# Second routed layer's rows and results in one DRAM buffer, sixteen early tiles, twenty stores on GpSimd, three gathers under way

## What is computed

```
raw_gate = softmax(einsum('btd,de->bte', x, gate))
_, topk_idx = top_k(raw_gate, 3)                      # of 16 experts
gate_topk = raw_gate where chosen, normed to sum 1
hidden = relu(einsum('btd,edh->bteh', x, W1) + b1)    # h = 256
expert_out = einsum('bteh,ehd->bted', hidden, W2) + b2
out = einsum('bte,bted->btd', gate_topk, expert_out)
x = x + out
```

## Time and profile before

| | us |
|---|---|
| median of 3 runs | 539.93 (538.46 to 541.28) |
| the profiled execution's own time | 540.01 |
| its span in the trace | 538.3 |
| PE busy | 415.3 (77%) |
| DVE busy | 336.5 (63%) |
| ACT busy | 240.1 (45%) |
| GpSimd (POOL) busy | 221.6 (41%) |

### The profile page before, as it was taken

The page is one execution under the profiler, slowest core; times in us unless marked ns, Lnnn a source line. Parts: engine busy times, 40 slices in busy tenths (PEclk is TensorE's granted clock), DMA queues, the critical chain, the costliest instruction groups (busy, mean ns, idle before and its releaser), DMA issues.

```text
span 538.3 us, 10062 instructions
## 1 busy us (share of the span) xinstructions
PE 415.3 (77%) x2628; PEld 344.9 (64%) x2628; DVE 336.5 (63%) x1143; ACT 240.1 (45%) x635; POOL 221.6 (41%) x276
## 2 busy tenths in 40 slices
PE   5887869999899888667899927763999999963450
PEld 5866758887676787357889915543767857752340
DVE  6656545654777767223444526667747588768887
ACT  1332316555344531444667713542566565742321
POOL 3511760035413777750215567554212254451215
PEclk9697559999798967577999968978999999995555
DMA  7999646892190111242336522110000000000002
GB/s 199 306 406 407 148 142 211 290 318 80 43 378 20 45 40 45 73 129 83 115 108 164 152 57 68 40 34 6 1 2 0 1 2 1 1 1 1 0 1 78
DMA packets 64421, 56.48 MB, mean 105 GB/s; under 512 B 12178, under 2 KB 50542, under 8 KB 64238
## 3 DMA queue, kind: packets, MB, share of 16 engines
q1 hardware_dynamic: 57534, 45.61, 25.9%
q0 software_dynamic: 4288, 8.79, 5.2%
q10 hardware_dynamic: 2544, 1.44, 0.9%
HBM read 24.10 MB, written 31.72 MB: 104 GB/s over the span
## 4 chain that ended last, share of the span: by engine, by line
PE 30%; DMA 18%; DVE 18%; POOL 13%; issue 10%; ACT 5%; DVEq 4%; SPq 1%; POOLq 0%; ACTq 0%
POOL rowbuf L645 8%; DMA vZ<-outbuf,slots 5%; PE bank L2104 4%; DMA rowbuf<-h_sb,slots 4%; PE bank L2250 4%; PE bank L2263 4%; DMA h_sb<-outbuf,slots 3%; PE bank L2120 3%; PE bank L2109 2%; POOL rstd L622 2%; PE bank L1959 2%; DMA wall<-outbuf,slots 2%; ACT xn L1631 2%; DVE stats L825 1%; DVE x L1285 1%
## 5 line engine op out<-in xcount | busy, mean ns | idle before, releaser
L1725 ACT ACTIVATE r<-bank,b 128x128 f32<-128x128 f32 x218 | 66.3, 366 | 36.1 <-PE bank L2250 35.3
L622 POOL TENSOR_TENSOR rstd<-veps,mhalf 128x4 f32<-128x4 f32 x32 | 33.8, 1057 | 110.4 <-DVE veps L830 110.1
L2263 PE MATMUL bank<-wall,r 128*128 x436 | 69.5, 293 | 11.9 <-DVE h_sb L1298 10.9
L645 POOL DMA_INDIRECT rowbuf<-h_sb,slots x64 | 63.0, 985 | 34.0 <-DMA rowbuf<-h_sb,slots 15.5
L2263 PEld LDWEIGHTS bank<-wall,r 128*128 128x128 f32 x436 | 59.1, 202 | 14.6 <-issue 12.8
L672 POOL DMA_INDIRECT vZ<-outbuf,slots x40 | 38.7, 968 | 60.5 <-DMA outbuf<-h_sb 35.8
L2250 PE MATMUL bank<-on,e_sb 128*128 128x128 f32 x348 | 58.4, 300 | 0.0
L2120 PE MATMUL bank<-vB,eT 128*128 128x36 f32 x384 | 50.8, 282 | 0.0
L2120 PEld LDWEIGHTS bank<-vB,eT 128*128 128x128 f32 x384 | 50.8, 206 | 0.0
L2250 PEld LDWEIGHTS bank<-on,e_sb 128*128 128x128 f32 x348 | 49.7, 210 | 0.1
L1298 DVE TENSOR_TENSOR h_sb<-bank,b2all 128x128 f32<-128x128 f32 x86 | 24.8, 290 | 38.0 <-PE bank L2263 36.4
(11 more groups left out here) (304 smaller groups left out, 840.1 us busy)
## 6 DMA issues: line engine op xcount, KB each, us to landing
outbuf<-zero SPq DMA_DIRECT2D x17, 1024.0 KB, 13.3
wall<-in_w SPq DMA_DIRECT2D x4, 2048.0 KB, 12.3
h_sb<-rowbuf SPq DMA_DIRECT2D x86, 64.0 KB, 2.1
outbuf<-h_sb SPq DMA_DIRECT2D x80, 64.0 KB, 2.1
rowbuf<-zero SPq DMA_DIRECT2D x24, 64.0 KB, 1.5
x<-in_x ACTq DMA_DIRECT2D x4, 256.0 KB, 5.6
rowbuf<-h_sb,slots POOLq DMA_INDIRECT x64, 2.2
b2all<-in_L_ffn_b SPq DMA_DIRECT2D x1, 1024.0 KB, 13.8
```

Of the source, the lines that this page charges most:

```text
L622: r = nc.gpsimd.tensor_tensor(rstd[:, at], veps[:, at], mhalf[:, 0:W], ALU.pow)
L645: placed = nc.gpsimd.indirect_dma_start(rowbuf[0:MOE[l][0] * REGION * P], bass.IndirectOffsetOnAxis(slots[:, k * T + t:k * T + t + 1], 0), ...
L1725: i = a.activation(hT[:, u * 512 + c * P:u * 512 + (c + 1) * P], bank[2 + u][:, c * P:(c + 1) * P], ACT.Relu, bias=b1[l][:, bass.ds(e * C ...
L2263: y = mm(bank[6 + s % 2][:, 0:P], hT[:, (s % 2) * 512 + c * P:(s % 2) * 512 + (c + 1) * P], wall[:, bass.ds(e * n + (WHALF + c * P), P)], ...
```

## The change

- In layer 3 the scattered rows go to `outbuf`, too (`rows_of[3]`): a slot's tile is loaded from there and its result is stored back to the same place. The zero tails of layer 3 fall away, since `outbuf` is cleared or holds finished rows of layer 1; before its first scatter of layer 3 GpSimd waits for layer 1's last gathers, the clears and `s_past`.
- `EARLY[3]` goes from 8 to 16, with `FROM[3]`, `LISTED[3]` and `TURNED[3]` later in step, and `PRIOR[3][0]` from 27 to 31.
- GpSimd stores slots 12 to 31 (20 of them) in place of 11, 13, ... 21 (6), and reads their list entries ten at a time.
- Layer 3's gathers wait for the third before them, not the second; scatters wait as before, with semaphores of their own.
- In layer 1, SP waits for the zero tails right after issuing them, ahead of the list read.

```diff
-PRIOR = {1: (11, 15, 19, 23), 3: (27, 39, 51, 63)}
-SHARE = range(11, 23, 2)
-EARLY = {1: 4, 3: 8}
+PRIOR = {1: (11, 15, 19, 23), 3: (31, 39, 51, 63)}
+SHARE = range(12, 32)
+UNDER_WAY = {1: 2, 3: 3}
+EARLY = {1: 4, 3: 16}
...
-FROM = {1: 3, 3: 4}
+FROM = {1: 3, 3: 8}
...
-LISTED = {1: (1, 2), 3: (1, 2)}
-TURNED = {1: 0, 3: 0}
+LISTED = {1: (1, 2), 3: (3, 6)}
+TURNED = {1: 0, 3: 4}
...
-        SCATTERS = {3: T * TOPK[1]}
-        GATHERS = {1: 0, 3: SCATTERS[3] + T * TOPK[3]}
-        def rows_landed(i):
-            return s_rows[i % 2], 16 * (i // 2 + 1)
-        def last_of(first, l, b):
-            return first[l] + (b + 1) * W * TOPK[l] - 1
+        def placed(n):
+            return s_scat[n % 2], 16 * (W + n // 2 + 1)
+        def gathered(l, n):
+            k = UNDER_WAY[l]
+            done = len(range(n % k, T * TOPK[1], UNDER_WAY[1])) if l == 3 and n % k < UNDER_WAY[1] else 0
+            return s_gat[n % k], 16 * (done + n // k + 1)
+        def last_of(l, b):
+            return (b + 1) * W * TOPK[l] - 1
...
+        rows_of = {1: rowbuf, 3: outbuf}
...
-                load(s_past, rowbuf[first:first + count * P].rearrange("(p r) f -> p r f", p=P),
+                load(s_past, rows_of[l][first:first + count * P].rearrange("(p r) f -> p r f", p=P),
...
-                        sp.wait_ge(s_sc1[i], 16 * W)
+                        sp.wait_ge(s_scat[i], 16 * W)
...
-                        sp.wait_ge(*rows_landed(last_of(SCATTERS, 3, b) - i))
-            def tile_load(at, s):
-                sp.dma_start(tile_of(xs, s % PLACES), rowbuf[bass.ds(at[s] * P, P)]).then_inc(s_xs[s % PLACES], 16)
+                        sp.wait_ge(*placed(last_of(3, b) - i))
+            def tile_load(l, at, s):
+                sp.dma_start(tile_of(xs, s % PLACES), rows_of[l][bass.ds(at[s] * P, P)]).then_inc(s_xs[s % PLACES], 16)
...
                     elif s == EARLY[l]:
-                        for row in zero_rows(l):
-                            zero_tail(l, row)
+                        if l == 1:
+                            for row in zero_rows():
+                                zero_tail(row)
+                            sp.wait_ge(s_zero, 16 * E)
                         sp.wait_ge(s_es, list_no(l) + 2)
...
                         scattered(l, 3)
-                        sp.wait_ge(s_zero[l], 16 * E)
                     elif s > EARLY[l] and s + AHEAD < SLOT_TILES[l]:
...
                             sp.wait_ge(s_xt, tb + s - PLACES + 1)
-                        tile_load(at, s)
+                        tile_load(l, at, s)
                     if s >= PLACES:
-                        if s == PLACES:
-                            sp.wait_ge(s_clr[l], loads[s_clr[l].name])
+                        if l == 1 and s == PLACES:
+                            sp.wait_ge(s_clr[1], loads[s_clr[1].name])
                         if l == 1 or not own_store(s - PLACES):
...
                             tile_store(at, s - PLACES)
...
                         t = b * W + w
-                        if l == 3:
-                            last_but_one_landed(SCATTERS[3] + t * TOPK[3] + k)
-                        placed = nc.gpsimd.indirect_dma_start(rowbuf[0:MOE[l][0] * REGION * P], bass.IndirectOffsetOnAxis(slots[:, k * T + t:k * T + t + 1], 0), tile_of(xn_all, t), None)
+                        n = t * TOPK[l] + k
+                        if l == 3 and n >= 2:
+                            pool.wait_ge(*placed(n - 2))
+                        i = nc.gpsimd.indirect_dma_start(rows_of[l][0:MOE[l][0] * REGION * P], bass.IndirectOffsetOnAxis(slots[:, k * T + t:k * T + t + 1], 0), tile_of(xn_all, t), None)
                         if l == 1:
-                            placed.then_inc(s_sc1[b], 16)
+                            i.then_inc(s_scat[b], 16)
                         else:
-                            placed.then_inc(s_rows[(SCATTERS[3] + t * TOPK[3] + k) % 2], 16)
-
-            def tile_store(s):
+                            i.then_inc(s_scat[n % 2], 16)
+
+            def tile_stores(first, last):
                 pool.wait_ge(s_es, list_no(3) + 2)
-                _, values = nc.values_load_multi_w_load_instructions(at_list[3][0:1, s:s + 1], engines=(mybir.EngineType.Pool,), min_val=0, max_val=NR - 1,
+                _, values = nc.values_load_multi_w_load_instructions(at_list[3][0:1, first:last], engines=(mybir.EngineType.Pool,), min_val=0, max_val=NR - 1,
                                                                      skip_runtime_bounds_check_because="one line of a segment is read for each slot")
-                if s == SHARE[0]:
-                    pool.wait_ge(s_clr[3], 16 * 8)
-                pool.wait_ge(s_yb, tile_before[3] + s + 1)
-                nc.gpsimd.dma_start(outbuf[bass.ds(values[0] * P, P)], tile_of(ys, s % PLACES)).then_inc(s_yp[s % PLACES], 16)
+                for s in range(first, last):
+                    pool.wait_ge(s_yb, tile_before[3] + s + 1)
+                    nc.gpsimd.dma_start(outbuf[bass.ds(values[s - first] * P, P)], tile_of(ys, s % PLACES)).then_inc(s_yp[s % PLACES], 16)
...
                     c = k * T + b * W + w
-                    i = GATHERS[l] + b * W * K + n
-                    last_but_one_landed(i)
-                    nc.gpsimd.indirect_dma_start(tile_of(yg[l][b], w * K + k), None, outbuf[0:MOE[l][0] * REGION * P], bass.IndirectOffsetOnAxis(slots[:, c:c + 1], 0)).then_inc(s_rows[i % 2], 16)
+                    i = b * W * K + n
+                    if i >= UNDER_WAY[l]:
+                        pool.wait_ge(*gathered(l, i - UNDER_WAY[l]))
+                    nc.gpsimd.indirect_dma_start(tile_of(yg[l][b], w * K + k), None, outbuf[0:MOE[l][0] * REGION * P], bass.IndirectOffsetOnAxis(slots[:, c:c + 1], 0)).then_inc(s_gat[i % UNDER_WAY[l]], 16)
...
             power(12)
+            for i in range(UNDER_WAY[1]):
+                pool.wait_ge(*gathered(1, last_of(1, 3) - i))
+            pool.wait_ge(s_clr[3], 16 * 8)
+            pool.wait_ge(s_past, loads["s_past"])
             for b in range(B):
...
                 scatter(3, b, (2, 3))
-            for s in SHARE:
-                tile_store(s)
+            for s in SHARE[::10]:
+                tile_stores(s, s + 10)
             gather(3, 0)
...
             gather(3, 2, 0, 3)
...
                 dve.drain()
-                for i in (1, 0):
-                    dve.wait_ge(*rows_landed(last_of(GATHERS, l, b) - i))
+                for i in range(UNDER_WAY[l]):
+                    dve.wait_ge(*gathered(l, last_of(l, b) - i))
                 if l == 1:
```

More of the change, by code:

```diff
@@ L165, in build @@
         lens = sb("lens", KINDS * SLOT_TILES[3], parts=16)
-        zero_at = {l: sb(f"zero_at{l}", 16, parts=1, dt=I32) for l in MOE}
+        zero_at = sb("zero_at", MOE[1][0], parts=1, dt=I32)
         reach = {l: sb(f"reach{l}", segs[l] + 2) for l in MOE}
@@ L289, in build @@
         s_gd = sem("s_gd")
-        s_zero = {l: sem(f"s_zero{l}") for l in MOE}
+        s_zero = sem("s_zero")
         s_past = sem("s_past")
@@ L299, in build @@
         s_b2l = sem("s_b2l")
-        s_rows = [sem("s_rows0"), sem("s_rows1")]
-        s_sc1 = [sem(f"s_sc1_{b}") for b in range(B)]
+        s_gat = [sem(f"s_gat{i}") for i in range(max(UNDER_WAY.values()))]
+        s_yp = [sem(f"s_yp{r}") for r in range(PLACES)]
+        s_scat = [sem(f"s_scat{b}") for b in range(B)]
         s_xs = [sem(f"s_xs{r}") for r in range(PLACES)]
@@ L310, in build @@
         s_ys = [sem(f"s_ys{r}") for r in range(PLACES)]
-        s_yp = {r: sem(f"s_yp{r}") for r in range(1, PLACES, 2)}
         s_gad = sem("s_gad")
@@ L518, in _, with zero_rows, zero_tail @@
             expert_biases(1)
-            def zero_rows(l):
-                E = MOE[l][0]
-                sp.wait_ge(s_za, 1 if l == 1 else 2)
-                _, values = nc.values_load_multi_w_load_instructions(zero_at[l][0:1, 0:E], engines=(mybir.EngineType.SP,), min_val=0, max_val=(NR - 1) * P,
+            def zero_rows():
+                sp.wait_ge(s_za, 1)
+                _, values = nc.values_load_multi_w_load_instructions(zero_at[0:1, :], engines=(mybir.EngineType.SP,), min_val=0, max_val=(NR - 1) * P,
                                                                      skip_runtime_bounds_check_because="a region is a tile longer than the rows that it can hold")
                 return values
-            def zero_tail(l, at):
-                sp.dma_start(rowbuf[bass.ds(at, P)], zero[:, 0:P]).then_inc(s_zero[l], 16)
+            def zero_tail(at):
+                sp.dma_start(rowbuf[bass.ds(at, P)], zero[:, 0:P]).then_inc(s_zero, 16)
             def tiles_of(l, first, last):
```

9 lines of the change are left out of this document (3 added, 6 removed).

## The result

| session (a chip each) | before, median us | changed kernel | ratio |
|---|---|---|---|
| first | 540.12 (538.46 to 541.28) | 524.0 (521.5 to 528.37) | 0.971 [0.964, 0.978] |
| second | 558.57 (550.58 to 570.49) | 570.21 (563.82 to 574.2) | 1.023 [1.014, 1.032] |
| third | 568.45 (563.23 to 570.7) | 576.7 (566.14 to 581.11) | none, see below |
| fourth | 536.16 (534.08 to 540.85) | not run; the same but for one wait in layer 1: 524.98 (520.32 to 526.19) | 0.979 [0.972, 0.987] |

In the session of the prediction the changed kernel takes 524.0 us, where 523.0 was forecast. In two of the three later sessions, on other chips, the kernel before is 18 to 28 us slower than in the first, and there the change doesn't gain: it loses 2.3% in the second.

A forecast was written before the change was run, and what follows sets the result against it. Layer 3 was taken to be bound by late tile loads and by the chain of slot 26's store, then 24 gathers, that DVE awaits at slot 59. 540.0 - 16.7 - 1.3 + 1.0 = 523.0 us, range 516 to 533.

The forecast's parts named there:

- First hole: Layer 3, PE's 8.23 us wait for slot 8's load: closes with sixteen early tiles if slot 16's load goes by 245.4.
- GpSimd's stores: Layer 3, slots 12 to 31: a store costs GpSimd 0.57 to 1.26 us, upper end taken; first gather 8.0 us earlier.
- the 272.7: Forecast start, in us, of layer 3's first gather, after slot 30's store lands at 271.7; it was 280.73 before.
- the start of the layer stays: Layer 3's beginning: sixteen early tiles need batches 0 to 2 only, as eight do, so no time changes there.
- The rival with stores at 2.67 us each: Layer 3: each GpSimd store waits for the last one's landing, first gather at 300.9; 551.2 us in all, chance 0.07.
- Three under way: Layer 3's 24 gathers take 28.75 plus 0.5 us; DVE goes on at slot 59 at 304.6, 16.7 us earlier.
- rival 1: Layer 3: the third gather brings nothing, the gathers' own DMA work sets 1.649 us each; 533.0 us, chance 0.12.
- the rival with a whole copy before each store: Layer 3: a 0.29 us DVE weight copy precedes each GpSimd store, first gather 5.5 us later; 528.5 us, chance 0.06.
- Batch 3: Layer 3's last seven gathers take 1.8 us less; 1.3 us of DVE's 1.72 us wait is taken as gain.
- Layer 1: SP's wait for the zero tails before the list read delays slot 4's load: cost 1.0 us, bounds 0 and 1.6.
- The term of layer 3: DVE goes on at its slot 59 at 304.6 instead of 321.28: 16.7 us gained.
- rival 3: Slower: layer 3's GpSimd stores go one at a time, each after the last one's landing; 551.2 us, chance 0.07.

The follow-up runs named there:

- the three depths above: Layer 3's gathers under way in the changed kernel: one 586.58 us (fourth session), two 554.88 (second) and 557.83 (third), three the changed kernel itself, 524.0 (first).
- the moved wait: Changed kernel with layer 1's wait for the zero tails moved back behind the list read: 524.98 us, 0.979 of the kernel before.
- the one run with 32 rows: Changed kernel with layer 3's gathers taking 32 of the 128 rows each, for timing only: 521.5 us.

## Why the prediction was right, and where it was not

*First hole.* Right. Slot 16's load went at 241.09 (forecast 242.6 to 243.7), as the last scatter, without the zero tails beside it, was issued 2.6 us sooner (1.1 of them because the first one was), and PE waited 0.77 and 0.55 us instead of 8.23.

*GpSimd's stores.* The mechanism was right and the price too high: four in 2.35 us are 0.6 each, not 1.26, the lower end of the bounds. But that price isn't in the 272.7: the forecast had the stores nearly keep DVE's pace with either. The first gather went at 269.96 because the tiles began sooner. Slot 5's bias came at 234.72 instead of 237.45: 1.1 of these 2.7 us were gained before layer 3, the other 1.6 in the scatters and the first tiles, where the forecast had put nothing ("the start of the layer stays"). From slot 5's bias to the first gather it took 35.24 us, and the forecast has 35.25. That this agrees so well is luck: slot 30's bias came 31.65 us behind slot 5's, not 31.0, and its store then went 0.65 us behind its end (at 267.31) instead of 0.92 and landed in 1.8 instead of 2.1. The list read that lies before slot 22's store shows as the 2.52 us at 259.67, and the four stores behind it made that up, as forecast. The rival with stores at 2.67 us each is out by the same row.

*Three under way.* 31.15 us for 24 gathers against 29.25: two of them waited 1.00 and 1.32 us, and a few took 1.1 us. With 2.7 gained and 1.9 lost DVE went on at 303.70 against 304.6. It had come there at 297.69, not 300.8, and so waited 6.01 us, not 3.8: the forecast was 3 us late with the tiles. That rival 1 (the third gather brings nothing) is out on this chip is shown by the spacing in the three depths above.

*DVE and GpSimd.* The trace doesn't bear out the rival with a whole copy before each store. The Trainium skill's rule (SBUF — State Buffer, the "DVE blocks DMA" trap) has a trace all the same: of the 22 copies L1310 between the first and the 24th gather, seven took 0.32 to 0.54 us instead of 0.29, and gathers up to 1.17 instead of 0.94. That is at most 0.25 us in each meeting, in one of three. The trace of the kernel before had it already, with copies of up to 0.52 and gathers of up to 1.07 where the forecast read 0.29 and 1.03 off the few rows it shows.

*Batch 3.* DVE's wait fell from 1.72 to 1.50 only, not by 1.3, and yet the last gathers did what was forecast: 7.63 us against 7.6. From the first of them to DVE's add it takes 10.12 us instead of 11.94, the 1.8 of the forecast; DVE came sooner as well. What is missing was lost ahead of them: 33.35 us instead of 32.39 from the add at slot 59 to the first of the seven, where PE's clock was 0.70 over the last 17 us and had been 0.95. *Layer 1.* Its 1.0 is borne out by the moved wait. The 2.3 us of layer 2's clock more than gave it back.

*Sum.* The term of layer 3 was 16.7, measured 16.5; batch 3 1.3, measured 0.9; layer 1 -1.0, measured +1.1 with the clock: 17.0 against 18.5. So the forecast time is met closely in part by luck: 2.3 us of the profiled execution are a clock that nobody forecast, and without them it would have taken 523.8.

*What was wrong.* The forecast took the tile pace of the earlier trace rows for a constant of the kernel. The trace of before gave no reason to doubt it, with 14 tiles in the first 15.3 us of its gathers. In two of the four sessions it isn't one: while gathers are issued the loop makes a tile in 3.8 us with three under way and in 1.7 with two. Per gather that is, over the twelve of batch 0 in the second session, (15.3 - 4 x 1.19) / 12 = 0.9 us with three, the halved clock included, and (18.0 - 10 x 1.19) / 12 = 0.5 with two. There the bound of the stage is the tile loop, the gathers wait for it, and a change that packs them closer loses. None of the rivals said this. The slower one, rival 3, has by chance the size seen in the second session (11.2 us slower forecast there, 11.6 measured), but its mechanism is out: GpSimd's stores went one a tile there too, the last three at 289.57, 290.77 and 291.95. So the forecast is right for the first session. In the fourth the time is within its range of 516 to 533, but the gain is 11.2 us, two thirds of the 17 forecast; without a trace of the kernel before in that session the difference stays open. In the other two the range doesn't hold.

*What stays open.* What holds the hand-overs while indirect DMAs are issued, and why in two sessions only. How the gain divides where there is one: eight early tiles, the old share of stores and two gathers were run in slow sessions only, so for a quick chip their parts are read from one trace and not shown by runs. Two gathers under way would lose, from the spacings (1.65 against 1.354), 23 x 0.3 = 7 us there, an estimate. In both slow sessions it is the quickest of all, against the kernel before by 0.2% (not told from nothing) and 1.4%.

## What to carry to other kernels

Where a queue of small DMAs is the chain that ends a stage, its price for each falls with the number under way, down to the issue floor of one instruction: here 2.97, 1.65 and 1.354 us for one, two and three, with a floor of 1.25. Dividing the price of one by the number is a lower bound only (2.97 / 2 = 1.49, where 1.65 was measured). Read both from the trace, and stop at the floor. Ask also what the loop beside it does while they are issued, and measure that on more than one chip: the same kernel was 2.9% faster on one and 2.3% slower on another. Where you can't, the smaller depth is the safer one here: by the estimate above it would give up 7 us on a quick chip, and it saved 15 on one of the slow ones.

## What the runs showed of the hardware

In two of four sessions, each on its own chip, work was handed between PE, ACT and DVE 1.5 to 2 us late while GpSimd issued indirect gathers or scatters, with the loads landed; the same hand-overs took about 0.2 us or less between the last scatter and the first gather. The last stage, without indirect DMAs, took 175.1 to 178.7 us in all four (179.6 in the one run with 32 rows). A 64 KB store issued by GpSimd costs it 0.54 to 0.6 us and lands in 2.0 (median of 20); an indirect gather costs 0.94 whether it takes 128 rows of 512 or of 32 bytes, and 0.86 for 32 rows.
